# Masks by kind, picked through registers, and a shorter chain to the softmax maxima in the opening of a two-layer mixture-of-experts kernel

## The reference, cut to what matters

```python
attn_in = jnp.tanh(jnp.einsum('bsd,da->bsa', hidden, W1) + b1)
scores = jnp.einsum('bsa,a->bs', attn_in, v)
prefix_m = l <= j
postfix_m = l >= j
cloze_m = l != j
mask = jnp.where(pt == 0, prefix_m[None], jnp.where(pt == 1, postfix_m[None], cloze_m[None]))
masked_scores = jnp.where(mask, scores[:, None, :], NEG_INF)
p = jax.nn.softmax(masked_scores, axis=-1)
cnt = jnp.sum(mask, axis=-1).astype(hidden.dtype)
pooled = jnp.einsum('bjl,bld->bjd', p, hidden) / cnt[..., None]
```

## Time and profile before

| | |
|---|---|
| time, median of 3 runs | 378.47 us (377.31 to 385.25) |
| the profiled execution: span | 377.3 us |
| the profiled execution: its own time | 377.3 us; no time outside the span is given, and the fastest of the three runs is 377.31 |
| PE busy | 345.8 us, 92% |
| DVE busy | 267.7 us, 71% |
| ACT busy | 239.5 us, 63% |
| POOL busy | 200.8 us, 53% |
| DMA | 41.07 MB, mean 109 GB/s |

### The profile page before, as it was taken

One profiled execution on the slowest core, in us unless ns is written; L12 is line 12 of the kernel. 1 busy time (PEld: TensorE's weight loads), 2 busy tenths in 40 slices (PEclk: granted clock), 3 DMA queues, 4 the chain that ended last, 5 costly groups with the idle time before them and its releaser, 6 DMA issues.

```text
span 377.3 us, 7373 instructions
## 1 busy us (share of the span) xinstructions
PE 345.8 (92%) x2130; PEld 202.0 (54%) x2131; DVE 267.7 (71%) x780; ACT 239.5 (63%) x423; POOL 200.8 (53%) x185
## 2 busy tenths in 40 slices
PE   8998999999999999789679888959999999999982
PEld 6676654444444454345345343437998997444430
DVE  0457738877739999889988849617699985356761
ACT  1456478778777666576566645709678888656550
POOL 5699999200007766446857846810216300478874
PEclk9999999999999999999999989979999999999999
DMA  7859932620056565334435100121334324631211
GB/s 206 263 127 356 406 112 68 164 65 0 3 140 141 147 125 124 82 88 104 114 93 139 59 0 17 46 83 30 95 105 128 101 60 99 160 84 43 64 55 56
DMA packets 47456, 41.07 MB, mean 109 GB/s; under 512 B 6850, under 2 KB 41522, under 8 KB 47290
## 3 DMA queue, kind: packets, MB, share of 16 engines
q1 hardware_dynamic: 44632, 36.25, 34.5%
q0 software_dynamic: 1760, 3.71, 3.3%
q10 hardware_dynamic: 1026, 0.65, 0.6%
HBM read 28.93 MB, written 11.67 MB: 108 GB/s over the span
## 4 chain that ended last, share of the span: by engine, by line
PE 45%; POOL 20%; DVE 11%; issue 10%; DMA 7%; ACT 2%; SPq 1%; POOLq 1%; ACTq 1%; DVEq 0%
PE bank L651 9%; POOL sorted_in L1767 7%; POOL whl L1855 6%; POOL acc L778 5%; PE bank L600 4%; PE bank L602 4%; PE bank L601 4%; DMA sorted_out<-yo 2%; DVE l L710 2%; PE bank L663 2%; PE bank L662 2%; PE bank L664 2%; PE bank L577 2%; DMA mg<-in_maskt 2%; PE bank L579 2%
## 5 line engine op out<-in xcount | busy, mean ns | idle before, releaser
L686 ACT ACTIVATE h<-bank,b1f 128x512 f32<-128x512 f32 x160 | 105.0, 687 | 77.3 <-PE bank L651 65.3
L710 DVE SCALAR_TENSOR_TENSOR l<-h 128x512 f16<-128x512 f32 x118 | 89.2, 759 | 20.0 <-ACT h L698 18.1
L778 POOL TENSOR_TENSOR acc<-acc,tmp 128x512 f32<-128x512 f32 x43 | 61.8, 1438 | 64.2 <-DVE tmp L751 57.9
L651 PE MATMUL bank<-h,w 128*128 128x512 f32 x160 | 82.6, 598 | 0.0
L698 ACT ACTIVATE h<-h 128x512 f16<-128x512 f32 x108 | 67.8, 628 | 2.7
L600 PE MATMUL bank<-xh,whl 128*128 128x512 f16 x128 | 48.8, 381 | 0.0
L602 PE MATMUL bank<-xh,whl 128*128 128x512 f16 x128 | 48.7, 381 | 0.0
L601 PE MATMUL bank<-xl,whl 128*128 128x512 f16 x128 | 48.7, 381 | 0.0
L1855 POOL DMA_INDIRECT whl<-sorted_out,idx x24 | 24.8, 1035 | 31.5 <-DMA sorted_out<-yo 25.2
L680 ACT ACTIVATE h<-bank,b1f 128x256 f32<-128x256 f32 x76 | 31.4, 468 | 9.7 <-PE bank L579 6.7
L1767 POOL DMA_INDIRECT sorted_in<-xs,idx x24 | 28.9, 1202 | 15.0 <-DVE idx L1675 9.1
(11 more groups left out here) (222 smaller groups left out, 675.9 us busy)
## 6 DMA issues: line engine op xcount, KB each, us to landing
Gs<-gates SPq DMA_DIRECT2D x40, 256.0 KB, 5.0
wraw<-in_w SPq DMA_DIRECT2D x16, 512.0 KB, 3.8
sorted_in<-zer SPq DMA_DIRECT2D x14, 448.0 KB, 6.7
wraw<-sorted_in SPq DMA_DIRECT2D x19, 128.0 KB, 2.2
sorted_out<-yo SPq DMA_DIRECT2D x19, 128.0 KB, 1.9
first<-in_xtm SPq DMA_DIRECT2D x1, 1024.0 KB, 7.8
mg<-in_gbc SPq DMA_DIRECT2D x8, 128.0 KB
w<-in_w SPq DMA_DIRECT2D x8, 128.0 KB, 2.7
```

Of the source, the lines that this page charges most:

```text
L651: pe.matmul(o[:, :], w2[:, e, j * 128:j * 128 + 128], h32[:, u % NH, :], start=(c == 0), stop=(c == 3))\
L686: act.activation(h32[:, u % NH, :], bank[u % 4][:, :], ACT.Gelu if layer else ACT.Gelu_apprx_tanh, bias=b1f[layer][:, e * 4 + c:e * 4 + c ...
L710: dve.scalar_tensor_tensor(l16[:, slot(u), :], h32[:, u % NH, :], HS, h16[:, slot(u), :], ALU.mult, ALU.subtract).then_inc(s_lo, 1)
L778: eng.tensor_tensor(a, a, tmp[:, i % NTMP, :], ALU.add).then_inc(s_acc, 1)
```

## The change

The three kinds of masks are loaded once, by one DMA of SP (3 x 128.5 KB); SP and POOL no longer read the types or fetch masks. PE and DVE read the 8 types themselves: `mask_kind` does it at its first call on each engine, with 8 `value_load`, and gives a register for the address of L1092's mask and of the counts in `norm`. On PE the first call stands in the argument of the third matmul of sequence 0, on DVE behind the wait for `p_po` in `norm(0)`.

In the chain to the maxima the scans read the scores directly from PSUM, with a constant row as second operand. PE computes the scores twice, into banks 4 and 6 (`p_sc` now counts three events); ACT writes `rows` from bank 6 and a second row `cl`, the scores plus an offset by type. DVE takes the maximum of `cl` with `pre` and with `suf`, each plus an offset of 0 or -1e30 by type: two mixing steps in place of four. The copy of `scol`, with `p_col`, now comes behind `p_m`.

```diff
-        maskt = mg[:, :].bitcast(BF16).rearrange("p (b n) -> p b n", b=B)
+        maskt = mg[:, 0:3 * 257].bitcast(BF16).rearrange("p (k n) -> p k n", k=3)
...
         def sp_loads(sp):
             sp.dma_start(w1c[:, :], t["w1c"]).then_inc(ld["c0"], 16)
             load_x(sp, 0)
             load_x(sp, 1)
-            sp.wait_ge(ld["ids"], 16)
-            for b in range(0, B, 2):
-                load_mask(sp, b)
+            sp.dma_start(maskt[:, :, :], t["maskt"].rearrange("k p c -> p k c")).then_inc(ld["mask"], 16)
             load_w(0)(sp)
...
         def pool_loads(pool):
             pool.wait_ge(t_zm, 1)
             pool.dma_start(selr[0:B, :], t["sel"]).then_inc(ld["sel"], 16)
-            pool.wait_ge(ld["ids"], 16)
-            for b in range(1, B, 2):
-                load_mask(pool, b)
...
+        def mask_kind(eng, name, b):
+
+            if name not in kinds:
+                eng.wait_ge(ld["ids"], 16)
+                kinds[name] = [eng.value_load(tyr[0:1, i:i + 1], min_val=0, max_val=2) for i in range(B)]
+            return bass.ds(kinds[name][b], 1)
...
-            for p in range(2):
-                last = pe.matmul(bank[4][0:B, 0:S], vz[:, p * B:p * B + B], attn[:, p * S:p * S + S],
-                                 start=(p == 0), stop=(p == 1))
-            last.then_inc(p_sc, 1)
+            for o in (bank[4], bank[6]):
+                for p in range(2):
+                    last = pe.matmul(o[0:B, 0:S], vz[:, p * B:p * B + B], attn[:, p * S:p * S + S],
+                                     start=(p == 0), stop=(p == 1))
+                last.then_inc(p_sc, 1)
...
-                pe.matmul(o, identb[:, :], maskt[:, b, 0:512], start=False, stop=True).then_inc(p_pm, 1)
+                pe.matmul(o, identb[:, :], maskt[:, mask_kind(pe, "pe", b), 0:512].rearrange("p a n -> p (a n)"),
+                          start=False, stop=True).then_inc(p_pm, 1)
...
-                ln(dve.tensor_tensor(rr[:, b % 2, 0, :], pb[:, D:512:256], maskt[:, b, 512:514], ALU.mult))
+                ln(dve.tensor_tensor(rr[:, b % 2, 0, :], pb[:, D:512:256],
+                                     maskt[:, mask_kind(dve, "dve", b), 512:514].rearrange("p a n -> p (a n)"), ALU.mult))
...
+            act.wait_ge(p_off, 1)
+            act.wait_ge(p_sc, 2)
+            act.activation(rows, bank[6][0:B, 0:S], ACT.Copy).then_inc(p_row, 1)
+            act.activation(cl[:, :], bank[6][0:B, 0:S], ACT.Identity, bias=off_t[:, 2:3]).then_inc(p_row, 1)
             act.wait_ge(p_col, 1)
...
+            sc, low = bank[4][0:B, 0:S], pre[:, 0:1].to_broadcast([B, S])
+            ln(dve.tensor_tensor_scan(pre[:, 1:S + 1], sc, low, -BIG, ALU.max, ALU.max))
+            ln(dve.tensor_tensor_scan(suf[:, S:0:-1], sc[:, ::-1], low, -BIG, ALU.max, ALU.max))
+            dve.wait_ge(p_row, 2)
+            ln(dve.scalar_tensor_tensor(cl[:, :], pre[:, 0:S], off_t[:, 1:2], cl[:, :], ALU.add, ALU.max))
+            ln(dve.scalar_tensor_tensor(mrow, suf[:, 2:S + 2], off_t[:, 0:1], cl[:, :], ALU.add, ALU.max))
             ln(dve.tensor_copy(mh[0:B, :], mrow))
             dve.tensor_tensor(ml[0:B, :], mrow, mh[0:B, :].bitcast(F32), ALU.subtract).then_inc(p_m, 1)
+            dve.wait_ge(p_sc, 3)
+            dve.tensor_copy(scol[:, :], bank[5][:, 0:NT]).then_inc(p_col, 1)
```

More of the change, by code:

```diff
@@ L181, in build_adaln_ffn @@
         tyr, lid = ids[:, 0:B], ids[:, B:2 * B]
-        is_t = sb("is_t", [B, 4])
+        off_t = sb("off_t", [B, 4])
         f0 = N + NT * (D + 1) + 8 * S
@@ L359, in build_adaln_ffn @@
         p_row = sem("p_row")
+        p_off = sem("p_off")
         p_lc = sem("p_lc")
@@ L947, in build_adaln_ffn @@
             load_sem(f"x{g}")
-        for b in range(B):
-            load_sem(f"mask{b}")
+        load_sem("mask")
         def load_x(eng, g):
             eng.dma_start(acc[:, g * 512:g * 512 + 512], t["xT"][:, g * 512:g * 512 + 512]).then_inc(ld[f"x{g}"], 16)
-        def load_mask(eng, b):
-            r = eng.value_load(tyr[0:1, b:b + 1], min_val=0, max_val=2)
-            eng.dma_start(maskt[:, b, :], t["maskt"][bass.ds(r, 1), :, :].rearrange("a p c -> p (a c)"))\
-                .then_inc(ld[f"mask{b}"], 16)
         def sp_loads(sp):
@@ L1046, in build_adaln_ffn @@
         EB = [0, 1, 2, 3, 4, 5, 4, 5]
+        kinds = {}
+        def mask_kind(eng, name, b):
[3 more added lines that the diff above has]
+            return bass.ds(kinds[name][b], 1)
         def warm(pe, n):
@@ L1082, in fn @@
                     pe.wait_ge(ld["identb"], 16)
-                pe.wait_ge(ld[f"mask{b}"], 16)
+                    pe.wait_ge(ld["mask"], 16)
                 if b == 5:
@@ L1215, in dve_prologue @@
             dve.wait_ge(ld["ty"], 16)
-            dve.tensor_scalar(is_t[:, 0:1], ty[:, :], 0.0, None, ALU.is_equal)
-            ln(dve.tensor_scalar(is_t[:, 1:2], ty[:, :], 1.0, None, ALU.is_equal))
-            ln(dve.tensor_tensor(is_t[:, 3:4], is_t[:, 0:1], is_t[:, 1:2], ALU.add))
-            ln(dve.tensor_scalar(is_t[:, 2:3], is_t[:, 3:4], -1.0, 1.0, ALU.mult, ALU.add))
+            for k in range(3):
+                last = dve.tensor_scalar(off_t[:, k:k + 1], ty[:, :], float(k), -BIG, ALU.is_equal, ALU.mult)
+            last.then_inc(p_off, 1)
+            dve.wait_ge(p_off, 1)
             dve.wait_ge(t_zm, 2)
             dve.wait_ge(p_sc, 1)
-            dve.tensor_copy(rows, bank[4][0:B, 0:S]).then_inc(p_row, 1)
-            dve.wait_ge(p_row, 1)
-            ln(dve.tensor_tensor_scan(pre[:, 1:S + 1], rows[:, :], rows[:, :], -BIG, ALU.max, ALU.max))
-            ln(dve.tensor_tensor_scan(suf[:, S:0:-1], rows[:, ::-1], rows[:, ::-1], -BIG, ALU.max, ALU.max))
-            dve.wait_ge(p_sc, 2)
-            dve.tensor_copy(scol[:, :], bank[5][:, 0:NT]).then_inc(p_col, 1)
-            ln(dve.tensor_tensor(cl[:, :], pre[:, 0:S], suf[:, 2:S + 2], ALU.max))
-            ln(dve.tensor_scalar(cl[:, :], cl[:, :], is_t[:, 2:3], None, ALU.mult))
-            ln(dve.scalar_tensor_tensor(cl[:, :], pre[:, 1:S + 1], is_t[:, 0:1], cl[:, :], ALU.mult, ALU.add))
-            ln(dve.scalar_tensor_tensor(mrow, suf[:, 1:S + 1], is_t[:, 1:2], cl[:, :], ALU.mult, ALU.add))
+            sc, low = bank[4][0:B, 0:S], pre[:, 0:1].to_broadcast([B, S])
[4 more added lines that the diff above has]
+            ln(dve.scalar_tensor_tensor(mrow, suf[:, 2:S + 2], off_t[:, 0:1], cl[:, :], ALU.add, ALU.max))
             ln(dve.tensor_copy(mh[0:B, :], mrow))
             dve.tensor_tensor(ml[0:B, :], mrow, mh[0:B, :].bitcast(F32), ALU.subtract).then_inc(p_m, 1)
+            dve.wait_ge(p_sc, 3)
+            dve.tensor_copy(scol[:, :], bank[5][:, 0:NT]).then_inc(p_col, 1)
         at("dve", -100, dve_prologue)
```

## The result

The changed kernel takes 399.24 us (median, 395.56 to 401.94), the kernel before 379.01 in the same comparison: ratio 1.052, 95% interval 1.047 to 1.058. It is slower by 20 us; 9.5 were forecast, and 388.0 us with a range up to 391.5. The profiled execution took 395.56 us with a span of 393.8, so 16.5 us of span more than before. That is the fastest of the changed kernel's six runs. Of the execution traced before only the span is on record, and in later executions of that kernel the time was 1.6 to 2.8 us above the span, so its time was about 379 us. Some 4 us of the difference of the medians are in runs that no trace shows.

A forecast was written before the change was run, and what follows sets the result against it. The prediction took PE's expert matmuls, started by the opening's chain, as the bound. Later start 6.6, first clock fall 2.5 and second 0.4 made 9.5 us, on a 378.5 us median 388.0, range 382 to 391.5.

The forecast's parts named there:

- Eight register loads on DVE: Between `pooled(0)` and `norm(0)`: serial loads from 23.5 to 28.4 us, 4.9 us, making `trans(0)` 7.1 us later.
- The clock, second fall: PE's idle time ahead of `trans(0)`, about 2.7 us, may bring half clock again; 0.4 us counted.
- the 0.5 I took off for a wait that would vanish: Between `trans(0)` and the first expert matmul: some 0.5 of the 4.23 us was a wait for ACT.
- The fall behind the first idle time: After PE idles about 4.2 us for its loads, half clock until `pooled(0)` ends: 2.5 us, bounds 0 and 3.2.
- The first softmax matmul: It would start at 15.1 us, when the selection matrix lands, between 14.5 and 15.5; 0.5 us gained.
- The chain itself: The shorter chain from scores to maxima would end at 14.5 us in place of 15.6, 1.1 us sooner.
- Eight register loads on PE: Between sequence 0's second and third matmul: 4.9 us serially, nothing hiding it, `pooled(0)` 3.3 us later.
- Carried to the end: A shift of the first expert matmul reaches the end one to one, as PE has no idle time from 45 to 150 us.
- half of the shift is taken up later: Rival, 13%: DVE's or POOL's own pace sets later waits, so 3 to 5 us of shift reach the end; 382.5 us.
- The rule against the trace: A waiting instruction holds PE's sequencer; by the skill's contrary rule loads start earlier, gaining at most 0.6 us, for 387.4.
- The loads cost more and the clock falls twice: Rival, 9%: 0.8 us per load, 1.5 us more on each engine, and 1 to 2 us more half clock; 392 us.

The follow-up runs named there:

- e5: The changed kernel with PE's eight registers read by one instruction ahead of the 62 warm matmuls, DVE's loads left in place; ratio 1.024 to the kernel before.
- e7: The changed kernel with SP's fills of zeros put behind position 20 of its queue, one execution; first expert matmul at 38.40 us.
- e14: The same kernel as e7, run six times; ratio 1.042 to the kernel before.
- e13: e5 with the first five of SP's fills of zeros put ahead of its fetches of constants, one execution; first expert matmul at 38.14 us.
- e9: The changed kernel with ten warm matmuls behind each of PE's loads and 130 ahead of the first transpose; 397.01 us, ratio 1.041.
- e10: The changed kernel with one early eight-register load per engine, the selection matrix fetched earlier and 24 warm matmuls in place of 62; ratio 1.002.
- e8: e10 with SP also waiting for the last part of x before it issues masks, weights and xtm; ratio 0.999 to the kernel before.
- e3: The changed kernel with DVE's eight register loads moved to the end of its opening; ratio 1.022 to the kernel before.
- e4: The changed kernel with DVE's loads at the end of its opening and PE's one eight-register load ahead of the warm matmuls; ratio 1.000.
- e6: The changed kernel with each engine's eight value loads replaced by one eight-register load at the same places; 382.36 us, ratio 1.005.

## Why the prediction was wrong

The direction and the mechanism were right: serial register loads on both engines, on the path on both, a fall of the clock, and the shift carried to the end. The size was under half of what came, and the time lies outside the range. In the span, 9.5 us were forecast and 16.5 came; at the first expert matmul 17.1. Of the 7.6 us by which the first expert matmul missed its forecast (36.1), 3.8 lie between DVE's first load and the norm, 2.8 between `trans(0)` and that matmul, and 0.9 ahead of `pooled(0)`.

*Eight register loads on DVE: the step that failed.* "They carry the wait for `p_po`" and start when `pooled(0)` is done: so it was (1.10 behind its start, as before). But "0.8 + 7 x 0.58 = 4.9 us" was taken over from SP, POOL and PE to a stretch of the program in which SP fills a buffer from SBUF. They took 8.7 us to the norm, 3.8 more; where no fills ran it was 5.3 (e5), so 3.4 of the 3.8 are the fills'. e7, e14 and e13 show that the fills are the cause, and that with what follows from the longer wait they are worth 4.5 to 5.2 us at the first expert matmul, 4 at the end. I had the row that could warn: the DMA engines at 370 GB/s from 27 to 45 us, the stretch into which I moved the loads. I used it for the price of bytes alone.

*The clock, second fall: mis-sized.* I gave the idle time before `trans(0)` 2.7 us and the fall 0.4, since "less is on the path". The idle time was 7.6, mostly because the loads were longer, and the lower level lasted until 46 us, over the whole of the 6.92 us from `trans(0)` to the first expert matmul (4.23 before). In e9, with the clock at 1.00, these two stand 4.82 apart (35.44, 40.26), so the lower level is worth 2.1 us, for a term for which 0.4 was set. The other 0.6 over the kernel before is there at full clock too, and the 0.5 I took off for a wait that would vanish didn't come. The fall behind the first idle time was there, as forecast: the exponents stood 1.3 apart in place of 0.66, and from the second sequence's first matmul to `pooled(0)` it took 3.87 us (21.90 to 25.77) where three exponents at 0.66 are 2.0: 1.9 for the 2.5 that I took.

*The first softmax matmul: wrong in sign.* 15.1 was forecast, and 16.55 came. The chain itself went as written: a scan from PSUM cost nothing extra, ACT's two rows were done at 13.1 (12.7 was the estimate), and the maxima were there at 14.97, for 14.5. Two things followed that I hadn't looked at. The warm row of 62 matmuls stands behind transposes that wait for `rows`, which ACT now writes 1.3 later (the transposes start at 12.90, 11.63 before), behind the second set of scores, so PE was busy with it until 16.5; I had counted it as filling and not as work in the queue. And the selection matrix came later, at 16.1, not sooner. POOL issues it behind a cast that waits for ident, and SP's fetches, no longer held back by register loads of their own, now run in front of ident (landed at 10.5, 8.1 before) and of the last part of x (8.4, 7.9 before). "Issued by POOL at the same place, behind the same work" was true of the queue and not of the time: 11.2 and not 8.9. e10 and e8 remove both and get the 0.05.

*Eight register loads on PE: right.* 4.9 us were forecast; the eight loads end at 21.4, 5.2 after they start, and the second sequence's matmuls came 4.7 later relative to the first. e3 and e5 show that these and DVE's have nearly the same weight at the end, where the sum gave 3.3 and 3.3 before the clock.

*Carried to the end: right, with some luck in how closely.* 17.1 at the first expert matmul, 17.6 at what stood at 150 us, 16.5 at the end. But from the first expert matmul to the end of the span it is 350.7 us before and 350.2 in the changed kernel, and in the other traces anything from 348.8 (e4) to 355.5 (e3). So a loss of this size reaches the end within some 5 us, and that the two differ by only 0.6 is luck. For small shifts it says little: e4 is 1.8 us late at that matmul and its ratio is 1.000, and in the other direction 2.2 us gained in e8 are not seen in the times. I gave "half of the shift is taken up later" 13%; in e4 and e8 all of it was.

*The rule against the trace.* PE's sequencer stood at L1082, a wait that is an instruction of its own, from 15.7 to 16.2, and the first load began at 16.25. That is 0.3 before the softmax matmul ahead of it started: this one had its semaphores, but stood in line behind the warm matmuls, and the sequencer read past it. In e6 that covered the whole load. So separate waits held the sequencer, and a matmul in line did not. The Trainium skill (Advanced Engine Details and Errata, Sequencer Loop) says that an engine instruction is pushed into a queue and the next one is read meanwhile; on this the trace agrees. It doesn't refute my "an instruction that waits holds the sequencer", which was about a matmul whose own semaphore is missing. On such a matmul only the earlier trace rows bear here, and by them the sequencer stood. The passing was worth 0.3 us.

*The rivals.* "The loads cost more and the clock falls twice" (9%, 392 us) was what happened, with 8.7 us on DVE in place of 6.4. Its price was taken from the dearest row of another engine (0.48 for a TENSOR_LOAD), so the range of the whole rested on a bound that no row of DVE supported.

## What to carry to other kernels

In this kernel a row of single register loads cost 0.65 to 0.7 us for each, serially, and up to twice that beside the fills out of SBUF. Read all registers of an engine by one instruction (0.8 us for eight), at a place where the engine waits anyway, not inside the argument of the first instruction that needs the value. When a register read or a DMA leaves a queue, look at what it was holding back: the fetches behind it now come early and in front of others. Before pricing a shorter chain, list everything that ends within a microsecond of it, warm filling matmuls included, since that is what the next bound will be.

## What the runs showed of the hardware

- A TENSOR_LOAD on DVE took 0.30 us, but mostly 0.65 to 1.53 while DMAs copied zeros out of SBUF (1.44, 1.06, 0.94, 0.90, 0.94 and then 0.30 in one row of e13). Moving the copies moved the slowness (e7, e14, e13).
- One load of eight registers took 0.78 to 0.79 us on PE and 0.84 on DVE; eight single ones 5.2 us on PE and 4.9 on DVE at best.
- A tensor_tensor_scan of 8x256 took 0.68 from PSUM and from SBUF.
- DVE's TENSOR_SCALAR of 128x256 into `xh` took 0.28 to 1.28 us; 43 of the 61 longer ones (0.45 and more) ended 0.14 to 0.15 us behind the POOL operation that ran beside them.
- Behind 4.65 us of idle time PE had 3.5 us at the lower clock; in an idle time of 7.6 us it fell to the lower one at 32.3 us and stayed there until 46, with PE busy for the last 9.3 of these (9.29 of 9.30).
